# Expert outputs stored by slot and gathered afterwards, with the middle phase run one chunk per step

## The chip, the cores and the metric

The kernel runs on one core of one Trainium2 chip. The metric is the device time of one execution in microseconds. The kernel is written by hand in a language that names each engine's instructions: TensorE (PE), VectorE (DVE), ScalarE (ACT), GpSimd (POOL) and SyncE (SP), each with its own order of instructions, joined by semaphores.

## The reference

Two transformer layers over `x` of 16 x 256 tokens with 128 channels, in float32. Each has attention and then a mixture of eight experts, both modulated by shifts, scales and gates computed from a conditioning vector. The part that matters here runs from the experts of the first layer to the start of the second layer's attention:

```python
h = _layernorm(x) * (1 + cb) + sb
x = x + gb * _L0_ffn_ref(h, ...)      # 8 experts, top 2, capacity 1280 per expert
h = _layernorm(x) * (1 + ca) + sa     # second layer's modulation
# _L1_attn_ref(h): q, k, v; an importance per token, of which the top 76 keys per
# sequence are kept:
Q, K, V = x @ wq.T + bq, x @ wk.T + bk, x @ wv.T + bv
importance = (relu(x @ wi1.T + bi1) @ wi2.T + bi2)[..., 0]
_, top_idx = jax.lax.top_k(importance, k)
```

In `_L0_ffn_ref` each token goes to its two best experts, `gelu(x W1 + b1) W2 + b2`, and its output is the sum of the two results by the router's weights.

## The kernel before

The kernel is a chain of phases, each a block in which all engines run and at whose end they meet: opening, relative attention, normalization and router tables, `route_phase`, `expert_phase`, `middle_phase`, sparse attention, then the second layer's `route_phase`, `expert_phase` and `final_phase`.

**Routing.** `route_phase` (from line 1752) gives each of the 8192 (token, choice) pairs a slot, so that the pairs of one expert stand together: 71 half tiles of 128 rows, of which 62 are taken in pairs, so 31 full tiles of 256 rows and nine half tiles, 40 tiles in all (`XTILES`). It keeps the slots as integers in `slot_i`, and derives two tables by half tile: `r.token`, the token of each row, and `r.dest`, where each row's output goes in `y_dram`, which is laid out by choice and token.

**Experts** (`expert_phase`, line 1979; the first layer's has `gated` false). For each tile j:
- POOL gathers its rows of `h_dram` by an indirect DMA per half (`gather`, line 2243) into one of eight places of `x_rows`, and scatters the output rows of tile j-1 to `y_dram` by one more per half (`scatter`, line 2253). In its loop the scatter of tile j-1 stands ahead of the gather of tile j+8.
- PE, in the order first layer of j+1, turning of j+2, second layer of j: eight matmuls of 256 columns (line 2071), transposes (line 2080), sixteen matmuls of 128 columns (line 2090).
- ACT applies gelu (line 2132), copies the turned rows (line 2140) and copies the next expert's weights into a ring (lines 2109 to 2111).
- DVE adds the output bias (`finish`, line 2178) and writes `y`, a ring of four. `y_free` makes it wait until the scatter of tile j-4 has landed.
- SP loads the middle's weights (`ahead`), the gates, waits until all scatters have landed (the semaphores `stored`), and issues the rows of the first two chunks of the middle (`choice_rows`, line 1973).

**Middle** (`middle_phase`, line 1078). Tokens are taken in eight chunks of 512 (`NCH`). `got` holds both choices' rows. SP loads them from `y_dram`, two plain DMAs of 256 KB per chunk. For a chunk, in this order:
- ACT weighs the first choice's rows into PSUM (`weigh`, line 1227) and DVE adds the second choice's (line 1314) into `both`.
- POOL multiplies by the gates (`gate`, line 1144), DVE adds to `x` (line 1296) and takes the statistics (lines 1301 and 1306).
- ACT's square root (line 1231), DVE's reciprocal and shift (lines 1320 and 1322), ACT's `normalize` (line 1239).
- PE transposes (`to_columns`, line 1169) and ACT's `modulate` (line 1248) writes the chunk's columns `hT`.
- PE: hidden layer (line 1175), queries (line 1179), keys and values (line 1184), importance (line 1190), and the importance turned to columns (line 1197), with ACT's `rectify` (line 1255), `queries` (line 1259) and `importance` (line 1264), and DVE's `keys_values` (line 1328) and `rank` (lines 1335 and 1341).

The order is written out by hand: a loop of `NCH + 5` steps in which each engine takes parts of up to five different chunks, so the chunks overlap. POOL also makes the tables `before`, `head_mask` and `places` here (lines 1147 to 1158), beside its gating.

## Time and profile before

| | us |
|---|---|
| median of 3 runs | 1309.27 |
| lowest and highest | 1299.88, 1310.76 |
| the profiled execution | 1304.45 |
| its span, first to last instruction | 1302.7 |
| mean granted TensorE clock, share of full | 0.911 |

The profile is one execution. Times in its views are microseconds from the start of its span. "Busy" counts an engine's instructions, without waits, branches and the issuing of DMAs, but an indirect DMA counts on POOL, which makes its descriptors. PEld is the loading of weights, which runs beside PE. A row's bracket says how long the engine was idle before it and who released it. The releaser is inferred from semaphores. "Remote" is one for which the profile has no name. Over the whole span PE is busy 79%, DVE 61%, ACT and POOL 60%.

### The profile page before, as it was taken

How to read it: one execution, taken by the hardware profiler on the slowest of the kernel's cores; microseconds unless marked ns; L12 is line 12 of the kernel's file. 1: busy time of each engine (PE TensorE's matmuls, PEld its weight loads, DVE VectorE, ACT ScalarE, POOL GpSimd, SP SyncE). 2: the span in 40 equal slices, each digit the busy share in tenths (PEclk: the TensorE clock that was granted, in tenths of full speed). 3: DMA queues.
4: the chain of work that ended last, by engine and by line, in shares of the span. 5: the costliest groups of instructions: out<-in, count | busy, mean ns of one | idle time of the engine just before them, and what ended most of it. 6: DMA issues, size and time to landing. Idle time of an engine off the chain costs nothing. (4 is left out here: it accounts for less than half of the span.)

```text
span 1302.7 us, 40110 instructions
## 1 busy us (share of the span) xinstructions
PE 1026.4 (79%) x16123; PEld 818.8 (63%) x16123; DVE 799.8 (61%) x1631; ACT 785.2 (60%) x1734; POOL 787.2 (60%) x807
## 2 busy tenths in 40 slices
PE   6788999999999647577677477899964787899970
PEld 4467777777777536567566433566643676788860
DVE  6578788888887585000000277699967545666765
ACT  5355555555555437345446685577753777788983
POOL 7566786877867402666656320788830366788764
PEclk9789999999999977898888889799986799999995
DMA  4733232323320162111111310200037111111117
GB/s 128 166 52 54 50 57 51 57 53 57 56 45 8 19 194 53 54 44 41 43 41 39 111 42 1 70 6 7 6 67 240 54 36 35 43 42 45 39 31 200
DMA packets 120840, 79.32 MB, mean 61 GB/s; under 512 B 44144, under 2 KB 111120, under 8 KB 120528
## 3 DMA queue, kind: packets, MB, share of 16 engines
q1 hardware_dynamic: 111568, 58.12, 19.6%
q0 software_dynamic: 9088, 18.63, 4.9%
q8 instruction: 129, 2.11, 0.7%
q14 instruction: 55, 0.45, 0.1%
HBM read 58.15 MB, written 17.76 MB: 58 GB/s over the span
## 5 line engine op out<-in xcount | busy, mean ns | idle before, releaser
L2071 PE MATMUL ps_h_x_m<-x_T_x_m,fc_x_m 128*128 128x256 f32 (+1 forms) x960 | 221.2, 384 | 77.8 <-issue 51.2
L2132 ACT ACTIVATE act_x_m<-ps_h_x_m,fc_bias_x_m 128x256 f32<-128x256 f32 (+1 forms) x480 | 181.5, 464 | 137.2 <-DMA q_dram<-qT 68.5
L2071 PEld LDWEIGHTS ps_h_x_m<-x_T_x_m,fc_x_m 128*128 128x128 f32 x960 | 175.3, 205 | 106.2 <-issue 85.5
L1027 ACT ACTIVATE probT<-ps_t 128x512 f32<-128x512 f32 (+1 forms) x208 | 118.7, 594 | 145.0 <-PE ps_t L855 143.8
L2253 POOL DMA_INDIRECT y_dram<-y_x_m,dest_m x142 | 144.5, 1018 | 94.4 <-DVE y_x_m L2178 44.7
L2243 POOL DMA_INDIRECT x_rows_x_m<-h_dram,token_m x142 | 141.8, 999 | 95.5 <-POOLq L1765 56.0
L2090 PE MATMUL ps_o_x_m<-proj_x_m,act_x_m 128*128 128x128 f32 x1136 | 145.5, 280 | 12.0 <-DVE act_x_m L2156 8.5
L2090 PEld LDWEIGHTS ps_o_x_m<-proj_x_m,act_x_m 128*128 128x128 f32 x1136 | 136.8, 196 | 15.8 <-DVE act_x_m L2156 10.9
L777 POOL TENSOR_TENSOR rel_y<-rel_raw,own_rows 128x1024 f32<-128x1024 f32 x64 | 130.4, 2040 | 26.7 <-ACT rel_raw L1035 26.6
L2178 DVE TENSOR_TENSOR y_x_m<-ps_o_x_m,out_rows_m 128x256 f32<-128x256 f32 (+1 forms) x40 | 15.8, 395 | 210.7 <-remote 155.6
L957 DVE TENSOR_REDUCE neg_max<-ps_s 128x8 f32<-128x512 f32 (+1 forms) x64 | 95.5, 1492 | 73.1 <-PE ps_s L840 72.8
L855 PE MATMUL ps_t<-ident,prob 128*128 128x128 f32 x640 | 96.0, 285 | 7.7 <-ACT prob L1020 7.0
L960 DVE TENSOR_TENSOR prob<-ps_s,neg_max 128x512 f32<-128x512 f32 (+1 forms) x64 | 95.4, 1491 | 2.2
L1020 ACT ACTIVATE prob<-prob 128x512 f32<-128x512 f32 (+1 forms) x64 | 81.4, 1272 | 22.6 <-DVE prob L960 22.5
L966 DVE TENSOR_REDUCE row_sum<-prob 128x8 f32<-128x512 f32 (+1 forms) x64 | 94.4, 1475 | 0.0
L855 PEld LDWEIGHTS ps_t<-ident,prob 128*128 128x128 f32 x640 | 69.1, 142 | 25.1 <-issue 11.2
L271 POOL TENSOR_TENSOR q_rel<-q_spread,t_mask 128x2048 f32<-128x2048 f32 x16 | 73.2, 4575 | 12.8 <-DMA q_spread<-q_dram 12.8
L840 PE MATMUL ps_s<-e_rel,q_rel 64*32 64x136 f32 (+13 forms) x4096 | 74.2, 260 | 7.7 <-issue 7.7
L791 POOL TENSOR_TENSOR inv_diag<-row_inv,own_query 128x1024 f32<-128x1024 f32 x16 | 30.6, 1914 | 77.2 <-DVE row_inv L970 77.2
L2109 ACT ACTIVATE fc_x_m<-fc_all_m 128x512 f32 (+1 forms) x80 | 69.3, 866 | 7.3 <-issue 5.2
L1598 ACT ACTIVATE probT<-ps_t 128x512 f32<-128x512 f32 (+1 forms) x96 | 53.8, 593 | 29.2 <-PE ps_t L1480 28.6
L828 PE MATMUL ps_s<-kT,q_diag 32*128 32x32 f32 (+7 forms) x1024 | 56.9, 336 | 17.0 <-DVE prob L960 12.1
(316 smaller groups left out, 2133.8 us busy)
## 6 DMA issues: line engine op xcount, KB each, us to landing
q_spread<-q_dram SPq DMA_DIRECT2D x256, 64.0 KB
got_m<-y_dram SPq DMA_DIRECT2D x32, 256.0 KB, 4.7
h_dram<-h_rows_m SPq DMA_DIRECT2D x16, 256.0 KB, 2.2
x_rows_x_m<-h_dram,token_m POOLq DMA_INDIRECT x142
y_dram<-y_x_m,dest_m POOLq DMA_INDIRECT x142
x<-L_attn_x SPq DMA_DIRECT2D x8, 256.0 KB, 4.1
q_dram<-qT SPq DMA_DIRECT2D x8, 256.0 KB, 10.5
gates<-gate_dram SPq DMA_DIRECT2D x16, 128.0 KB, 4.2
```

Of the source, the lines that this page charges most:

```text
L777: pool.tensor_tensor(view(rel_y[:, u % 3, 4 * (m % 2), 0, :], 0, [[16, 4 * H], [4, 4], [1, 4]]), view(rel_raw[:, m % 3, :], 0, [[4, 4 * H] ...
L855: x = pe.transpose(ps_t[:, t % 2, p * P:(p + 1) * P], prob[:, m % 2, p, u * P:(u + 1) * P], k.ident[:, :])
L957: dve.tensor_reduce(neg_max[:, m % 2, :, :], split(ps_s[:, 0, :], m), AX.X, ALU.max, negate=True).then_inc(maxed, 1)
L960: dve.tensor_tensor(split(prob[:, m % 2, 0, :], m), split(ps_s[:, 0, :], m), view(neg_max[:, m % 2, :, :], 0, [[2, GROUPS], [1, 2], [0, n] ...
L966: dve.tensor_reduce(row_sum[:, b % 2, :, 2 * j:2 * j + 2], split(prob[:, m % 2, 0, :], m), AX.X, ALU.add).then_inc(summed, 1)
L1020: act.activation(p_, p_, ACT.Exp).then_inc(expd, 1)
L1027: act.activation(probT[to:to + n, store(m, ch), :, (2 * j + s) % 4, :], ps_t[row:row + n, t % 2, :].rearrange("p (g c) -> p g c", g=GROUPS ...
L2071: m = pe.matmul(ps_h[:, l, g, f % 2, 0:w], fc[:, slot, l, f * P:(f + 1) * P], x_T[:, slot % 2, 0:w], start=True, stop=True)
L2090: m = pe.matmul(ps_o[:, s % 2, h * P:(h + 1) * P], act1[:, s % 2, f, h * P:(h + 1) * P], proj[:, s, f, :], start=f == 0, stop=f == FK - 1)
L2132: m = act.activation(out[:, slot % 2, f, 0:w], ps_h[:, l, g, f % 2, 0:w], ACT.Tanh if l else ACT.Gelu, scale=0.5 if l else 1.0, bias=fc_bi ...
L2243: pool.indirect_dma_start(out=x_rows[:, slot, h, :], out_offset=None, in_=k.h_dram, in_offset=bass.IndirectOffsetOnAxis(ap=r.token[:, c:c ...
L2253: pool.indirect_dma_start(out=k.y_dram, out_offset=bass.IndirectOffsetOnAxis(ap=r.dest[:, c:c + 1], axis=0), in_=y[:, slot, h, :], in_offs ...
```

## The change

It does five things.

1. In the first experts POOL's scatters go. A new DRAM tensor `y_slots` holds the outputs by slot, and SP stores each tile there by a plain DMA once DVE has written it. `y_free` waits for those stores. POOL's gather of tile j+8 now waits until PE has turned tile j.
2. In the middle, POOL gathers the rows of each chunk from `y_slots` by the slots in `r.slot`, one indirect DMA per 128 tokens and choice: eight per chunk, 64 in all. SP's loads of them go, those ahead of the block's end too.
3. DVE multiplies by the gates, in place of POOL.
4. The loop of the middle has `NCH + 1` steps: in one step each engine takes chunk i from the weighing to its modulated columns, and beside it chunk i-1 from the hidden layer to the ranks.
5. POOL makes the tables at the end of the experts' phase, after the last tile is turned.

The second layer's experts and the final phase keep the scatters and the loads.

```diff
-        STEPS = NCH + 5
+        STEPS = NCH + 1
...
-        @block.sync
-        def _(sp):
-            for n in range(LEAD, NCH):
-                choice_rows(sp, k, r, n)
...
-            def gate(n):
-                pool.wait_ge(both_ready, 4 * (n + 1))
-                if n == 0:
-                    pool.wait_ge(gates_in, 16)
-                y = view(both[:, n % 2, 0, :], 0, [[2 * C, 2], [C, 2], [1, C]])
-                pool.tensor_tensor(y, y, view(gates[:, 2 * n, :], 0, [[C, 2], [0, 2], [1, C]]), ALU.mult).then_inc(gated, 1)
...
+            def choices(n):
+                for t in range(4 * n, 4 * n + 4):
+                    for c in range(TOPK):
+                        pool.indirect_dma_start(out=got[:, c, t, :], out_offset=None, in_=k.y_slots,
+                                                in_offset=bass.IndirectOffsetOnAxis(ap=r.slot[:, c * NT + t:c * NT + t + 1], axis=0)
+                                                ).then_inc(rows_in[n], 16)
+
+            for n in range(NCH):
+                choices(n)
...
             for i in range(STEPS):
-                if i == 3:
+                if i == 1:
                     pe.wait_ge(w_copied, 3)
                     pe.wait_ge(wi2_ready, 1)
-                if chunk(i - 3):
-                    hidden(i - 3)
-                    queries(i - 3)
-                if chunk(i - 2):
-                    to_columns(i - 2)
-                if chunk(i - 4):
-                    columns(i - 4)
-                if chunk(i - 3):
-                    keys_values(i - 3, 0)
-                    importance(i - 3)
-                if chunk(i - 3):
-                    keys_values(i - 3, 1)
+                if chunk(i - 1):
+                    hidden(i - 1)
+                    queries(i - 1)
+                    keys_values(i - 1, 0)
+                    importance(i - 1)
+                    keys_values(i - 1, 1)
+                    columns(i - 1)
+                if chunk(i):
+                    to_columns(i)
...
-                act.wait_ge(rows_in[n], 16 * TOPK)
+                act.wait_ge(rows_in[n], 16 * TOPK * 4)
...
-            weigh(0)
-            weigh(1)
             act.wait_ge(bq_ready, 1)
             for i in range(STEPS):
-                if chunk(i - 3):
-                    rectify(i - 3)
                 if chunk(i - 1):
-                    deviation(i - 1)
-                if chunk(i - 3):
-                    queries(i - 3)
-                if chunk(i - 2):
-                    modulate(i - 2)
+                    rectify(i - 1)
+                    queries(i - 1)
+                if chunk(i):
+                    weigh(i)
                 if chunk(i - 1):
-                    normalize(i - 1)
-                if chunk(i - 3):
-                    importance(i - 3)
-                if chunk(i + 2):
-                    weigh(i + 2)
+                    importance(i - 1)
+                if chunk(i):
+                    deviation(i)
+                    normalize(i)
+                    modulate(i)
             act.activation(warm[:, :], k.eps[:, 0:1], ACT.Exp)
 
         @block.vector
         def _(dve):
             def statistics(n):
+                dve.wait_ge(both_ready, 4 * (n + 1))
+                if n == 0:
+                    dve.wait_ge(gates_in, 16)
+                y = view(both[:, n % 2, 0, :], 0, [[2 * C, 2], [C, 2], [1, C]])
+                dve.tensor_tensor(y, y, view(gates[:, 2 * n, :], 0, [[C, 2], [0, 2], [1, C]]), ALU.mult).then_inc(gated, 1)
                 dve.wait_ge(gated, n + 1)
                 xs = k.x[:, 4 * n:4 * n + 4, :]
...
-            weigh(0)
             for i in range(STEPS):
                 if chunk(i - 1):
-                    statistics(i - 1)
-                if chunk(i - 4):
-                    keys_values(i - 4, 1)
+                    keys_values(i - 1, 0)
+                if chunk(i):
+                    weigh(i)
+                    statistics(i)
                 if chunk(i - 1):
-                    invert(i - 1)
-                if chunk(i - 5):
-                    rank(i - 5)
-                if chunk(i + 1):
-                    weigh(i + 1)
-                if chunk(i - 3):
-                    keys_values(i - 3, 0)
+                    keys_values(i - 1, 1)
+                if chunk(i):
+                    invert(i)
+                if chunk(i - 1):
+                    rank(i - 1)
...
-        slot_i, part_i = sb("slot_i", [P, KT], I32), sb("part_i", [P, 2, KT], I32)
+        slot_i, part_i = r.slot, sb("part_i", [P, 2, KT], I32)
...
+        def arrived(j):
+
+            return moved(j) if gated else count(j) if j >= 0 else 0
...
+            for j in range(0 if gated else XTILES):
+                sp.wait_ge(y_ready, j + 1)
+                c, n = first_half(j), halves(j)
+                sp.dma_start(k.y_slots[c * P:(c + n) * P, :].rearrange("(h p) c -> p h c", p=P),
+                             y[:, j % UNROLL, 0:n, :]).then_inc(stored[j % UNROLL], 16)
             for i in range(UNROLL):
-                sp.wait_ge(stored[i], 16 * moved(XTILES - 1 - (XTILES - 1 - i) % UNROLL))
-            for n in range(LEAD):
+                sp.wait_ge(stored[i], 16 * arrived(XTILES - 1 - (XTILES - 1 - i) % UNROLL))
+            for n in range(LEAD if gated else 0):
                 choice_rows(sp, k, r, n)
...
-                wait(dve, stored[j % UNROLL], 16 * moved(j - UNROLL))
+                wait(dve, stored[j % UNROLL], 16 * arrived(j - UNROLL))
...
             for j in range(XTILES + 1):
-                if not gated and exists(j - 1):
-                    scatter(j - 1)
...
-                    elif j == 0:
+                    else:
                         pool.wait_ge(x_turned, j + 1)
                         pool.nop(nofuse=True)
                     gather(j + ROWS)
                 if gated and exists(j - 1):
                     scatter(j - 1)
+            if r.tables:
+                pool.wait_ge(x_turned, XTILES)
+                pool.nop(nofuse=True)
+                r.tables(pool)
 
```

The edits left out move the table code unchanged into `middle_tables`, allocate `y_slots`, `r.slot` and the tables' tiles, and pass `tables` through.

## Rows read from the trace of the kernel before

**Rows 1.** Busy time by stretch, all engines: first experts, middle, second experts late.

```profile
core 0: us, PE busy (x) PEld busy (x) DVE busy (x) ACT busy (x) POOL busy (x), PEclk, DMA share, GB/s
508.00:536.00 28.00, 14.98 (x64) 12.24 (x64) 0.42 (x1) 10.20 (x26) 17.32 (x18) 0.70 0.36 96
536.00:660.00 124.00, 85.14 (x497) 75.49 (x497) 8.07 (x19) 59.74 (x156) 78.78 (x80) 0.87 0.15 43
...
760.00:813.00 53.00, 45.86 (x169) 22.50 (x167) 41.11 (x160) 36.70 (x80) 5.09 (x4) 0.98 0.00 1
1199.00:1233.00 34.00, 32.48 (x209) 29.57 (x208) 24.84 (x74) 30.30 (x73) 26.89 (x28) 1.00 0.13 41
...
```

**Rows 2.** Waits between 505 and 737 us: who waited for whom, total, times, longest.

```profile
DVE y_x_m L2178 <- remote: 155.6, 19, 27.5
ACT act_x_m L2132 <- DMA q_dram<-qT: 68.5, 19, 6.5
...
POOL y_dram L2253 <- DVE y_x_m L2178: 44.7, 17, 4.9
...
```

**Rows 3.** Timeline at the start of the first experts (start, us, engine, line).

```profile
521.17 1.95 PE L2090 MATMUL ps_o_x_m<-proj_x_m,act_x_m 128*128 128x128 f32 x16
...
530.40 0.94 POOL L2243 DMA_INDIRECT x_rows_x_m<-h_dram,token_m  x1 [0.30 <-issue]
...
535.01 0.42 DVE L2178 TENSOR_TENSOR y_x_m<-ps_o_x_m,out_rows_m 128x256 f32<-128x256 f32 x1 [27.45 <-remote]
...
```

**Rows 4.** Timeline, two consecutive first layers of full tiles.

```profile
594.13 1.89 PE L2071 MATMUL ps_h_x_m<-x_T_x_m,fc_x_m 128*128 128x256 f32 x8
...
597.86 1.89 PE L2071 MATMUL ps_h_x_m<-x_T_x_m,fc_x_m 128*128 128x256 f32 x8
...
```

**Rows 5.** Timeline of DVE, the outputs of tiles 1, 20, 29, 30 and 39.

```profile
536.29 0.42 DVE L2178 TENSOR_TENSOR y_x_m<-ps_o_x_m,out_rows_m 128x256 f32<-128x256 f32 x1 [0.85 <-PE ps_o_x_m L2090]
...
660.60 0.43 DVE L2178 TENSOR_TENSOR y_x_m<-ps_o_x_m,out_rows_m 128x256 f32<-128x256 f32 x1 [8.33 <-remote]
...
705.94 0.42 DVE L2178 TENSOR_TENSOR y_x_m<-ps_o_x_m,out_rows_m 128x256 f32<-128x256 f32 x1 [6.53 <-remote]
712.54 0.42 DVE L2178 TENSOR_TENSOR y_x_m<-ps_o_x_m,out_rows_m 128x256 f32<-128x256 f32 x1 [6.18 <-remote]
...
733.75 0.29 DVE L2178 TENSOR_TENSOR y_x_m<-ps_o_x_m,out_rows_m 128x128 f32<-128x128 f32 x1 [0.81 <-PE ps_o_x_m L2090]
...
```

**Rows 6.** Timeline: the second gather of the first tile, and TensorE on that tile.

```profile
510.38 0.95 POOL L2243 DMA_INDIRECT x_rows_x_m<-h_dram,token_m  x1 [0.30 <-issue]
...
512.96 0.69 PE L2080 MATMUL ps_x_x_m<-ident,x_rows_x_m 128*128 128x128 f32 x2 [7.22 <-DMA x_rows_x_m<-h_dram,token_m]
...
```

**Rows 7.** Timeline, the middle's first instructions and first chunks.

```profile
740.87 1.09 PE L1201 MATMUL ps_q<-ident,w_rows 128*128 128x128 f32 x4 [7.35 <-PEq L1988]
...
742.94 2.41 ACT L1227 ACTIVATE ps_part<-got_m,weight_m 128x128 f32<-128x128 f32 x8
...
749.74 1.65 ACT L1239 ACTIVATE normed<-x,shift,rstd 128x128 f32<-128x128 f32 x4 [0.44 <-DVE shift L1322]
...
756.43 1.94 PE L1175 MATMUL ps_i<-hT,wi_T 128*64 128x512 f32 x2 [3.88 <-ACT hT L1248]
...
```

**Rows 8.** Timeline, the middle's last chunks.

```profile
796.68 1.07 PE L1175 MATMUL ps_i<-hT,wi_T 128*64 128x512 f32 x2
...
798.85 0.69 ACT L1259 ACTIVATE qT<-ps_q,bq 128x512 f32<-128x512 f32 x1 [0.37 <-PE ps_q L1179]
...
799.43 1.01 ACT L1248 ACTIVATE hT<-ps_out,mod 128x256 f32<-128x256 f32 x2
...
802.69 1.07 PE L1175 MATMUL ps_i<-hT,wi_T 128*64 128x512 f32 x2
...
812.41 0.48 DVE L1341 SCALAR_TENSOR_TENSOR compared<-imp_row,imp_col,before 128x256 f32<-128x256 f32 x1
...
```

**Rows 9.** The page's DMA issues: KB each, median us to landing.

```profile
h_dram<-h_rows_m SPq DMA_DIRECT2D x16, 256.0 KB, 2.2
...
```

More of the change, by code:

```diff
@@ L1075, with middle_tables @@
 TINY = 2.0 ** -126
+def middle_tables(pool, a):
+    step = Chain(pool, a.table_step)
+    before = a.before
+    step(pool.memset(before[:, :, :], -TINY))
+    step(pool.affine_select(out=before[:, :, :], in_=before[:, :, :], compare_op=ALU.is_gt, fill=0.0, base=0,
+                            pattern=[[P, 2], [-1, T]], channel_multiplier=1))
+    step(pool.memset(a.head_mask[:, :], 1.0))
+    for p in range(4):
+        m = a.head_mask[4 * HD * p:4 * HD * (p + 1), :]
+        step(pool.affine_select(out=m, in_=m, compare_op=ALU.is_ge, fill=0.0, base=0,
+                                pattern=[[-HD, 4]], channel_multiplier=1))
+        step(pool.affine_select(out=m, in_=m, compare_op=ALU.is_ge, fill=0.0, base=HD - 1,
+                                pattern=[[HD, 4]], channel_multiplier=-1))
+    pool.iota(a.places[:, :], [[1, KEPT]], base=0, channel_multiplier=0,
+              allow_small_or_imprecise_dtypes=True).then_inc(a.tables_ready, 1)
 def middle_phase(nc, k, r, a):
@@ L2342, in _, with experts @@
             sp.wait_ge(stored, 16 * NCH)
-def experts(nc, d, k, name, layer, gate_w, gate_b, capacity, weights, gated, ahead, then):
+def experts(nc, d, k, name, layer, gate_w, gate_b, capacity, weights, gated, ahead, tables, then):
     with ExitStack() as ctx:
@@ L2374, in experts, with layer0_experts @@
         then(r)
-def layer0_experts(nc, d, k, ahead, then):
+def layer0_experts(nc, d, k, ahead, tables, then):
     w = Place()
@@ L2381, in layer0_experts @@
     w.rows = [d["L0_ffn_proj_bias"]]
-    experts(nc, d, k, "_m0", 0, d["L0_ffn_gate_w"], None, CAPACITY, w, False, ahead, then)
+    experts(nc, d, k, "_m0", 0, d["L0_ffn_gate_w"], None, CAPACITY, w, False, ahead, tables, then)
 def layers_between(nc, d, k):
@@ L2410, in then, with tables @@
                 middle_phase(nc, k, r, a)
-            layer0_experts(nc, d, k, ahead, then)
+            def tables(pool):
+                middle_tables(pool, a)
+            layer0_experts(nc, d, k, ahead, tables, then)
             clear_semaphores(nc, k)
```

31 lines of the change are left out of this document (10 added, 21 removed).

## The prediction, made before the changed kernel was built or run

> **What bounds the kernel now.** I read the busy time by stretch first. The first experts run from 508 to 736 us, the middle from 741 to 813 us. Between 536 and 660 us no engine is full: PE 85 of 124 us, ACT 60, POOL 79, DVE 8 [rows 1]. So the stage is held by waits, and the table of waits comes next: DVE waits 155.6 us for the second layer, under a releaser the profile cannot name, ACT 68.5 us before its activations (also under an impossible name), and POOL 44.7 us for DVE [rows 2]. POOL, whose scatters the change removes, itself waits in this stage, so its 1.0 us issues are not simply the bound.
>
> The timeline shows what is late. TensorE's 16 second-layer matmuls of tile 0 stand at 521.17 to 523.12 us, yet DVE starts on their result only at 535.01, after 27.45 us of idleness; POOL's row of gathers ended at 531.34 [rows 3]. The results of TensorE reach their readers late while POOL issues indirect DMAs back to back, and arrive together soon after POOL falls idle. In the middle, where POOL issues none, ACT's copy of the queries starts 2.17 us after the hidden layer's matmuls began, and those and the queries' own take all of it [rows 8]. That is a reading of times, not a proof. Two facts set the scale. Undisturbed, a full tile takes 597.86 - 594.13 = 3.73 us of PE [rows 4]. In fact 29 tiles take 712.54 - 536.29 = 176.3 us, or 6.08 each; between 660.60 and 705.94 nine take 5.04 each [rows 5]. POOL's four issues per full tile (two gathers, two scatters) cost 4 x 1.3 = 5.2 us: 78.78/80 = 0.98 busy each [rows 1] and 0.30 between [rows 3]. So scatters cost in two ways: they set a floor of 5.2 us, and they keep POOL busy without a break.
>
> **First experts: what the scatters' going brings.** 71 scatters leave POOL. Per full tile it has 2 x 1.25 = 2.5 us of work [rows 3, 6], under PE's 3.73. The stores go to SP, 40 plain DMAs of 64 or 128 KB. A plain store of 256 KB lands in 2.2 us [rows 9]; the output ring has four slots, some 15 us, so DVE does not wait. SP has the middle's weights and the gates ahead of them, and they are issued by 517 us, before tile 0's output exists. The added wait for x_turned before each gather binds little: POOL is eight tiles ahead.
>
> How near to 3.73 does a tile come? The nearest case is late in the second experts (1199 to 1233 us), where a tile has three indirect DMAs instead of four: PE is busy 32.48 of 34 us at full granted clock, while POOL is busy 26.89 of it [rows 1]. So with pauses in POOL's stream the lateness goes. Bounds: 3.73 (PE's own work) and 6.08 (nothing gained). I take 4.1, near the first, since some lateness may stay. The first 28 us, sixteen gathers back to back, stay as they are. Tile 1's output still ends at 536.7, then 29 x 4.1 = 118.9, then nine half tiles as before, 733.75 - 712.54 = 21.2: the last output ends at 676.8 instead of 734.04. That is -57.3 us.
>
> **Between the stages.** Before: last output 734.04, first instruction of the middle 740.84 [rows 5, 7], with a scatter, its landing and four loads issued by SP. After: a store of 2.2 us and the same barrier, about 4.5 us until POOL issues.
>
> **Middle: what comes instead.** Rows no longer arrive by eight-tile loads of 256 KB. POOL issues 64 gathers, eight per chunk, 1.25 us each with the gap: 10 us per chunk, 80 us in all. A gather begun at 510.38 is used by PE at 512.96 [rows 6], so a chunk's rows are there 7 x 1.25 + 2.6 = 11.3 us after its first issue. The first chunk pays all of it.
>
> The second half of the change sets the pace, though. Everything from weighing to the modulated columns of a chunk is now one step, and ACT weighs the next chunk only behind rectify and queries of the one before. Its length: from the first weighing (742.94) to the last normalization (751.39) is 8.45 us [rows 7]. POOL's gating of 1.3 us in it becomes a DVE operation of 0.7, leaving 7.9; transposes 0.6 and modulation 1.01 [rows 8] with hops make 9.6. Before ACT weighs again come hidden and queries matmuls and the queries copy: 796.68 to 799.54 [rows 8], with a hop 3.0 us. Period: 12.6 us, more than POOL's 10. Before, chunks overlapped over five steps at about 6.1 us (802.69 - 796.68 = 6.0 between two chunks' hidden layers [rows 8]).
>
> That is at full clock. PE's work per chunk, about 45.86/53 of the old 6.1 us [rows 1], 5.3 us, or somewhat more, is then under half of the time. Where PE was busy 15 of 28 us (508 to 536) the granted clock was 0.70, against 0.98 in the old middle, busy 46 of 53 [rows 1]. At 1.2 GHz the hidden layer's matmuls take 1.94 us instead of 1.07 [rows 7, 8], the queries' the same, the key and value copy that stands before DVE's weighing comes later and the transposes double: about +3.0, a period of 15.6. Between 12.6 and 15.6 I take 14.0.
>
> The Trainium skill (TensorE: Matmul & The Clock Gate, HAM oscillation) says that short bursts of matmuls with waits between them keep falling back to half rate. By that rule the period would be 15.6 throughout, and the sum 11 us above mine. The 0.70 row above agrees with it in part: the clock there was neither full nor half.
>
> Sum of the middle from the last output: 4.5 + 11.3 + 9.6 (0.4 more at half clock, 10.0) + 7 x 14.0 = 98 + the tail from the last chunk's hidden layer to the last rank, which took 802.69 to 812.89 = 10.2 before [rows 8] and has no other chunk beside it now, 8.7: 132.5 us. Before it was 812.89 - 734.04 = 78.9. That is +53.6 us.
>
> **What costs nothing.** The mask tables, about 4 us of POOL in the old middle, go to the end of the experts' stage, where POOL waits for PE anyway; their reader, the first rank, comes over 30 us later, and without that cover they would delay the first gather by 4 us. DVE's eight gatings, 8 x 0.7, are in the period. The second experts and the final phase keep their path.
>
> **The sum.** The profiled execution took 1304.45 us (span 1302.7), 4.8 below the median of 1309.27, within the three runs. 1304.45 - 57.3 + 53.6 = 1300.8; as the median lies higher I name 1303.
>
> **Rivals.**
> *PE's results come late in the middle too (slower).* POOL now issues 64 gathers without a break, just the pattern of 508 to 531 us [rows 3]. A chunk has three results of PE on its critical way (transposes, hidden, queries). For: the lateness stood beside unbroken gathers, with no scatter. Against: until 520 us, with PE at half clock and few matmuls, nothing was late, and the middle is sparser still. Price: 2.7 us each makes a period of 22 for the 80 us of issuing, so 2.7 chunks by then after the first; the other 4.3 at 14 give 4.5 + 80 + 60 + 8.7 = 153, +74 us, total 1321; at 5 us each (period 29) 163, +84, total 1331. It outweighs the gain from 1.2 us a chunk on. I take 1327.
> *Both at their floors (faster).* Tiles at 3.75: last output at 666.7, -67.4. Full clock in the middle: 4.5 + 11.3 + 9.6 + 88.2 + 8.5 = 122.1, +43.2. Total 1280. For: the late second experts [rows 1]. Against: the 0.70 row.
> *The experts gain nothing (the change does not do what it says).* If what holds PE is not POOL's issuing, tiles stay at 6.08 and only the middle's 54 us remain: 1356. Against it stands the late second experts.
>
> **Chances.** Forecast 0.45 (its own range 1283 to 1325), late results in the middle 0.27, both floors 0.25, no gain 0.03. The range 1268 to 1342 holds the first three with their spread. A measurement of this kernel tells about 1% from no change. Faster by over 1%: all of both floors and 0.11 of the forecast, 0.36. Slower by over 1%: 0.24 of the late results, 0.03 of no gain and 0.09 of the forecast, 0.36. Within 1%: 0.28.
>
> **What would show it.** Outputs of the first experts every 4 us and the last near 677 us; POOL idle between pairs of gathers; PE's clock near 1 there. In the middle, 64 gathers at 1.25 us, ACT's weighing every 14 us and not every 10, a granted clock near 0.75, and the last rank about 132 us after the last output. I am wrong if tiles stay above 5 us, if the middle follows POOL's 10 us, or if DVE and ACT there wait for PE long after its matmuls.

## The result, and the profile after: slower by 3.7%

The changed kernel takes 1351.8 us (median of 4 runs, 1346.4 to 1357.1) against 1304.6 us for the kernel before on the same chip (4 runs): ratio 1.037, 95% interval 1.032 to 1.042. The forecast was 1303 in a range of 1268 to 1342. The profiled execution took 1355.9 us, span 1353.8, against a span of 1302.7 before. Ratios and their intervals leave out the executions that were over 1.5% above the fastest of the same kernel.

First the busy time by stretch of the changed kernel, in the columns of [rows 1]:

```profile
core 0: us, PE busy (x) PEld busy (x) DVE busy (x) ACT busy (x) POOL busy (x), PEclk, DMA share, GB/s
536.00:660.00 124.00, 117.42 (x811) 109.21 (x811) 13.74 (x33) 96.96 (x261) 48.56 (x52) 0.95 0.24 62
...
700.00:740.00 40.00, 8.72 (x22) 4.03 (x22) 7.26 (x27) 5.62 (x14) 30.24 (x33) 0.59 0.20 52
...
780.00:820.00 40.00, 21.88 (x61) 10.33 (x60) 20.99 (x81) 16.61 (x39) 0.00 (x0) 0.71 0.00 0
820.00:860.00 40.00, 24.85 (x62) 10.98 (x61) 17.28 (x65) 15.84 (x33) 0.00 (x0) 0.73 0.00 1
```

Two opposite stories. From 536 to 660 us TensorE is busy 117.4 of 124 us, where it was 85.1 [rows 1]: the first experts now run at PE's own pace. From 700 to 740 us it is busy 8.7 of 40, ACT 5.6 and DVE 7.3. Only POOL is at work, with its gathers end to end, 30.24 us busy: one begins every 1.25 us, 0.95 of it busy and 0.30 between. That is the middle, and no other engine does much in it.

The outputs of the first experts on DVE, the first three, two in a row later, and the last (compare [rows 3, 5]):

```profile
542.95 0.42 DVE L2179 TENSOR_TENSOR y_x_m<-ps_o_x_m,out_rows_m 128x256 f32<-128x256 f32 x1 [32.89 <-remote]
543.90 0.42 DVE L2179 TENSOR_TENSOR y_x_m<-ps_o_x_m,out_rows_m 128x256 f32<-128x256 f32 x1 [0.52 <-PE ps_o_x_m L2091]
550.44 0.42 DVE L2179 TENSOR_TENSOR y_x_m<-ps_o_x_m,out_rows_m 128x256 f32<-128x256 f32 x1 [6.12 <-PE ps_o_x_m L2091]
...
565.41 0.42 DVE L2179 TENSOR_TENSOR y_x_m<-ps_o_x_m,out_rows_m 128x256 f32<-128x256 f32 x1 [3.31 <-PE ps_o_x_m L2091]
569.14 0.42 DVE L2179 TENSOR_TENSOR y_x_m<-ps_o_x_m,out_rows_m 128x256 f32<-128x256 f32 x1 [3.31 <-PE ps_o_x_m L2091]
...
673.02 0.29 DVE L2179 TENSOR_TENSOR y_x_m<-ps_o_x_m,out_rows_m 128x128 f32<-128x128 f32 x1 [0.81 <-PE ps_o_x_m L2091]
```

The first output is 7.9 us later than before (542.95 against 535.01), and soon a full tile takes 3.73 us, exactly PE's own work in [rows 4]. The last output ends at 673.31 instead of 734.04: 60.7 us gained. This is one execution: seven later kernels with the same first experts give their first output at 535.7 to 539.6 us and their last at 667.5 to 670.4, so differences of up to 7 us here are no effect of an edit.

The middle gives it back. In the table of waits, 676 to 770 us (the stretch in which POOL gathers, and 11 us more):

```profile
PE ps_out L1166 <- issue: 30.4, 2, 18.5
DVE kv L1322 <- remote: 30.3, 1, 30.3
...
DVE kv L1322 <- issue: 20.4, 2, 11.3
...
ACT hT L1242 <- issue: 19.7, 1, 19.7
PE ps_i L1172 <- ACT hT L1242: 19.6, 1, 19.6
...
ACT imp_row L1258 <- remote: 16.4, 2, 11.5
```

Single waits of 10 to 30 us, under releasers that explain nothing ("remote", "issue"). The timeline shows what three of them waited for:

```profile
705.58 1.12 PE L1187 MATMUL ps_i<-hid,wi_rep 64*128 64x512 f32 x2
...
711.44 0.69 ACT L1258 ACTIVATE imp_row<-ps_i,bi 128x512 f32<-128x512 f32 x1 [4.90 <-remote]
...
712.18 0.58 PE L1194 MATMUL ps_col<-ident,imp_row 1*128 1x1 f32 x4 [4.41 <-ACT imp_row L1258]
...
724.63 1.12 PE L1166 MATMUL ps_out<-ident,normed 128*128 128x128 f32 x4 [11.87 <-issue]
733.12 0.16 DVE L1329 COPY imp_col<-ps_col 128x4 f32<-128x4 f32 x1 [10.22 <-remote]
...
744.33 1.02 ACT L1242 ACTIVATE hT<-ps_out,mod 128x256 f32<-128x256 f32 x2 [19.75 <-issue]
```

TensorE's matmuls for the importance are over at 706.7, and ACT copies the result 4.7 us later. The four turned columns are over at 712.8 and DVE takes them at 733.1, 20 us later, though only 10.2 of these are its wait for them. The four transposes of the next chunk are over at 725.8, and ACT modulates them at 744.3, 18.6 us later. These are the late results of [rows 3], now in a stage where one chain of such results is all there is.

Two more of them stand in the way of the chunks, the keys and values:

```profile
706.63 1.13 PE L1181 MATMUL ps_kv<-w_T,hT 128*128 128x256 f32 x4
...
721.93 0.69 DVE L1322 TENSOR_TENSOR kv<-ps_kv,bkv 128x512 f32<-128x512 f32 x1 [11.29 <-issue]
...
749.16 1.03 PE L1181 MATMUL ps_kv<-w_T,hT 128*128 128x256 f32 x4
...
765.36 0.69 DVE L1322 TENSOR_TENSOR kv<-ps_kv,bkv 128x512 f32<-128x512 f32 x1 [30.25 <-remote]
```

In the one-step order DVE inverts the deviation of chunk i only behind the second half of the keys and values of chunk i-1, and adds the rows of chunk i only behind their first half. The second half, over at 707.8, is read at 721.93, after a wait of 11.3 us. The first half of the next chunk, over at 750.2, is read at 765.36, 15 us later.

The last gather ends at 759.3 us. The last late results are read at 765.4 and 768.9 (DVE's keys and values, ACT's importance), and from then on the lateness is gone. ACT on the next chunks:

```profile
785.84 1.65 ACT L1233 ACTIVATE normed<-x,shift,rstd 128x128 f32<-128x128 f32 x4 [0.56 <-DVE shift L1316]
788.70 1.02 ACT L1242 ACTIVATE hT<-ps_out,mod 128x256 f32<-128x256 f32 x2 [1.21 <-PE ps_out L1166]
```

Modulation waits 1.21 us for the transposes and chunks follow each other every 14.9 us. The eight modulations start at 699.58, 744.33, 773.76, 788.70, 803.46, 818.66, 833.47 and 848.03. So the second chunk took 44.8 us, the third 29.4, and the other five 14.9 each.

The page's groups and DMA issues for the new operations:

```profile
L1153 POOL DMA_INDIRECT got_m<-y_slots,slot_m x64 | 60.9, 952 | 26.0 <-issue 19.2
...
y_slots<-y_x_m SPq DMA_DIRECT2D x31, 128.0 KB, 1.9
```

The middle lasts 186.3 us from the last output to the last rank, which ends at 859.63; before it was 78.9. So the stage gives 107 us away for the 60.7 won. With 4 us more in the second experts (from the first gather to DVE's last reading of TensorE's output 245.6 instead of 241.7) that is the span's 51 us.

### The profile page after: what moved, and what is told of

The parts are those of the page before. It is cut to its first block and busy times, and to the rows that moved or that the text cites. A ratio compares the mean times of both kernels' runs of the same rounds, so it can differ in the third digit from the quotient of the medians.

```text
span 1353.8 us, 40121 instructions
## 1 busy us (share of the span) xinstructions
PE 1036.4 (77%) x16123; PEld 821.0 (61%) x16123; DVE 803.4 (59%) x1639; ACT 787.6 (58%) x1734; POOL 764.5 (56%) x792
## 5 line engine op out<-in xcount | busy, mean ns | idle before, releaser
L2072 PE MATMUL ps_h_x_m<-x_T_x_m,fc_x_m 128*128 128x256 f32 (+1 forms) x960 | 210.6, 371 | 25.1 <-issue 22.7
L1027 ACT ACTIVATE probT<-ps_t 128x512 f32<-128x512 f32 (+1 forms) x208 | 118.8, 594 | 146.5 <-PE ps_t L855 145.3
L2072 PEld LDWEIGHTS ps_h_x_m<-x_T_x_m,fc_x_m 128*128 128x128 f32 x960 | 169.4, 198 | 49.7 <-issue 30.9
L2254 POOL DMA_INDIRECT y_dram<-y_x_m,dest_m x71 | 72.6, 1023 | 29.6 <-issue 21.5
L1153 POOL DMA_INDIRECT got_m<-y_slots,slot_m x64 | 60.9, 952 | 26.0 <-issue 19.2
L1618 POOL TENSOR_SCALAR select<-places,rank 128x76 f32<-128x76 f32 x32 | 14.9, 479 | 102.1 <-POOLq L61 102.1
```

Source lines behind the costliest of these rows:

```text
L1027: act.activation(probT[to:to + n, store(m, ch), :, (2 * j + s) % 4, :], ps_t[row:row + n, t % 2, :].rearrange("p (g c) -> p g c", g=GROUPS ...
L2072: m = pe.matmul(ps_h[:, l, g, f % 2, 0:w], fc[:, slot, l, f * P:(f + 1) * P], x_T[:, slot % 2, 0:w], start=True, stop=True)
```

## The experiments

Theory L: while POOL issues indirect DMAs back to back, TensorE's results reach their readers late. The rivals: the one-step order of the middle is the cost (O), the middle merely waits for its rows (W), a busy POOL is enough, whatever it does (B). Kernels e1 to f4 and g1 ran once each, g2 to g4 six to ten times. All kernels are measured by three points that the timeline shows: the last output of the first experts, the last rank, and between them the middle.

**e1: the middle's rows by plain loads.** POOL's 64 gathers go, SP loads in their place.

```diff
-            for n in range(NCH):
-                choices(n)
...
+            for n in range(NCH):
+                for c in range(TOPK):
+                    first = 4 * n + c
+                    sp.dma_start(got[:, c, 4 * n:4 * n + 4, :],
+                                 k.y_slots.rearrange("(n p) c -> p n c", p=P)[:, first:first + 4, :]).then_inc(rows_in[n], 16)
```

> Edit: the changed kernel, but the middle's rows come by 16 plain loads of SP from y_slots instead of 64 gathers of POOL (so it leaves out the choice of the rows; amount and layout are the same). The one-step order and DVE's gates stay. Theory L (TensorE's results reach their readers late while POOL issues gathers back to back): no late results in the middle, weighing of the first chunk some 8 us after the last output, then 14.5 to 15 us a chunk, middle 125 to 135 us from the last output to the last rank instead of 186, total 1290 to 1300 (after is 1352). Rival O (the one-step order itself makes the middle long): middle stays at 165 us or more, total above 1330.

Measured: 1285.7 us (before 1297.4 on the same chip, one execution each), 4 under my range; the middle takes 133.3 us, within it. No result is late: "remote" releases nobody, and all eight modulations wait 1.2 us. Chunks follow every 14.8 us on average from the first to the last. O falls as the whole cause: 53.0 us of the 186.3 have gone with POOL's gathers. About 8 of these are no late result: the first modulation starts 17.9 us after the last output instead of 26.3, since the first rows come sooner. This kernel leaves out the choice of the rows, and so do e2, f2 and f3: they price a part and are no versions to use.

**e2: as e1, in the old order.**

```diff
-        STEPS = NCH + 1
+        STEPS = NCH + 5
...
-                    statistics(i)
+                    statistics(i - 1)
```

(and so on for the three engines, as the kernel before has it; DVE keeps the gates.)

> Edit: as e1, and the middle's engines in the order of the kernel before (13 steps), DVE keeps the gates. Theory L: middle about as before (79 us, up to 85 with the gates on DVE), total 1240 to 1252: the experts' gain alone, 55 to 65 us below before. Against e1 it prices the one-step order at some 50 us. Rival O would put 90 us or more between e1 and e2.

Measured: 1232.2 us, 65 us under before and 8 under the lowest I had named. The middle takes 79.6 us, as before (78.9), so DVE's gates cost nothing that shows. Against e1 the one-step order costs 53.7 us. The granted clock was lower in it; how much of the 53.7 us that makes, no run shows. The stretch 700 to 740 us of e1:

```profile
700.00:740.00 40.00, 25.39 (x63) 11.36 (x62) 17.60 (x63) 16.49 (x37) 0.00 (x0) 0.70 0.00 0
```

TensorE is busy 25.4 of 40 us at a granted clock of 0.70, against 45.9 of 53 at 0.98 in the old middle [rows 1].

So the ledger of the changed kernel's middle is: 79.6 (old order, plain rows), + 53.7 (one-step order), + 53.0 (POOL's gathers) = 186.3 us. The parts depend on the order in which they are added: by way of e3 below, the gathers are 63.6 and the one-step order 43.1.

**e3: POOL's gathers, old order.** The edit of e2 made to the changed kernel itself.

```diff
-        STEPS = NCH + 1
+        STEPS = NCH + 5
```

> Edit: the changed kernel with POOL's 64 gathers, but the middle's engines in the order of the kernel before (13 steps). If the gathers only set a pace (10 us a chunk, last rows 86 us after the last output, then the old order's tail of 25 to 30 us): middle 111 to 116, total 1277 to 1285. Theory L: late results as well, so middle 120 to 160, total 1286 to 1325, with waits on results that had long been computed in the first 80 us. Rival O: as the pace alone.

Measured: 1299.8 us; middle 143.2 us, in the range of L and 27 above the most that the pace of the gathers allows. Its modulations show it: they start at 718.30, 739.69, 764.85, then every 6 to 8 us. With these gathers the old order is no rescue; it ends level with the kernel before.

The trace of e3 also shows that theory L is too narrow. Here DVE waits late for results of its own:

```profile
719.76 0.68 DVE L1295 TENSOR_TENSOR both<-both,gates_m 128x512 f32<-128x512 f32 x1
...
726.33 0.69 DVE L1298 TENSOR_TENSOR x<-x,both 128x512 f32<-128x512 f32 x1 [5.89 <-remote]
```

The addition needs only the product, over at 720.44, and starts 5.9 us later. The next chunk has the same (6.7 us), and the moments come 4.7 us after their statistics twice. In e1, e4 and f1 none of these waits is above 0.6 us.

**e4: slower gathers.**

```diff
                 for t in range(4 * n, 4 * n + 4):
                     for c in range(TOPK):
...
+                    idle_step(pool.memset(idle[:, :], 0.0))
```

> Edit: the changed kernel, with a memset of POOL (128x1152, by the trace's memsets about 1.05 us) after each pair of gathers, so that a pair takes 3.6 us as in the first experts, where no result was late; 64 gathers then take 115 instead of 80 us. Theory L (back to back is what counts): no late results, chunks at 14.5 to 15 us, last rank about 146 us after the last output instead of 186, total 1307 to 1318: slower gathers make the kernel faster. Rival G (any gather delays results): late results over the whole 115 us, total 1352 or more. Rival O: 1345 to 1365.

POOL in e4, and the busy time of a stretch:

```profile
700.42 0.94 POOL L1157 DMA_INDIRECT got_m<-y_slots,slot_m  x1 [0.30 <-issue]
701.37 1.07 POOL L1160 MEMSET idle_p<- 128x1152 f32 x1
702.71 0.95 POOL L1157 DMA_INDIRECT got_m<-y_slots,slot_m  x1 [0.27 <-POOL idle_p L1160]
```

```profile
700.00:740.00 40.00, 24.11 (x62) 10.99 (x60) 19.42 (x73) 16.15 (x37) 33.36 (x35) 0.71 0.14 37
```

Measured: 1300.6 us, 51 below the changed kernel's median, and a middle of 144.4 us instead of 186.3. A pair of gathers takes 3.54 us, of which 1.3 are free of gathers; the same gathers take 113 us instead of 80, POOL is even busier, and TensorE does 24.1 us of work in the stretch in which it did 8.7. No wait is named "remote", and chunks follow every 14.9 us. The 11 us over e1's middle are all ahead of the first modulation (29.4 us after the last output, against 17.9), where the first rows are awaited. It is the plainest evidence for L: making the suspect slower makes the kernel faster. It was 6 us faster than the lowest I had named, 4.8 of it because the last output came at 668.5 instead of 673.3 (it stands at 667.5 to 670.4 in the seven kernels of this section with the same experts).

**f2: gathers that nobody reads.** Beside e1's plain loads POOL does this:

```diff
+        @block.gpsimd
+        def _(pool):
+            for t in range(NT):
+                if t == NT // 2:
+                    pool.wait_ge(unread_in, 16 * TOPK * t)
+                for c in range(TOPK):
+                    pool.indirect_dma_start(out=unread[:, c, t % (NT // 2), :], out_offset=None, in_=k.y_slots,
+                                            in_offset=bass.IndirectOffsetOnAxis(ap=r.slot[:, c * NT + t:c * NT + t + 1], axis=0)
+                                            ).then_inc(unread_in, 16)
```

> Edit: e1 (rows by plain loads, one-step order), and beside it POOL issues 64 gathers of the same rows, back to back, into a buffer that nobody reads (one short wait after the 32nd, since the buffer holds half). Nothing in the middle depends on them, so what they cost is what issuing them does to others. Theory L: results late again while POOL issues, middle 175 to 190 us instead of 133, total 1325 to 1345. Rival W (the changed kernel's middle waited for its rows): middle 133 to 140, total 1286 to 1293.

The waits of f2, 676 to 800 us:

```profile
DVE kv L1331 <- remote: 46.2, 3, 30.9
...
ACT hT L1251 <- remote: 19.8, 1, 19.8
...
DVE imp_col L1338 <- remote: 11.4, 2, 10.3
```

and its second chunk, TensorE's transposes and the modulation that reads them:

```profile
706.63 1.11 PE L1175 MATMUL ps_out<-ident,normed 128*128 128x128 f32 x4 [9.49 <-ACT normed L1242]
```

```profile
726.35 1.02 ACT L1251 ACTIVATE hT<-ps_out,mod 128x256 f32<-128x256 f32 x2 [19.77 <-remote]
```

Measured: 1347.1 us, 2 over my range, and a middle of 182.9 us against e1's 133.3. The rows are there as early as in e1, and nothing in the middle depends on POOL. Still the transposes, over at 707.7, are read at 726.4. W falls: gathers that nobody waits for, with the rows in place, cost 49.6 us.

**f3: a busy POOL without gathers.** Beside e1's plain loads, memsets of 128x1024:

```diff
+            for _ in range(80):
+                idle_step(pool.memset(idle[:, :], 0.0))
```

> Edit: e1, and beside it POOL does 80 memsets (128x1024, by the trace's memsets some 0.9 us each) one after the other, some 80 us, and no gather. Theory L (the issue of indirect DMAs is what delays): middle 133 to 137, total 1284 to 1291. Rival B (a busy POOL is enough): middle 160 or more, total above 1310.

The stretch 700 to 740 us, as shown of e1:

```profile
700.00:740.00 40.00, 26.54 (x66) 11.97 (x66) 16.63 (x62) 16.51 (x37) 37.70 (x41) 0.67 0.00 0
```

Measured: 1288.0 us, middle 133.0 us, the same as e1's 133.3, with POOL busy 37.7 of 40 us. B falls. It is the indirect DMAs, not POOL being busy.

Two rivals had no run of their own, but the traces bear on them. *The traffic of the gathers*: between 536 and 660 us of the changed kernel, where outputs are read on time, the DMA engines' share is 0.24 at 62 GB/s; between 700 and 740, where they are not, it is 0.20 at 52. So the amount moved is not the cause by itself; whether it is the making of the descriptors or the small packets that come without a break stays open. *Loading of the engines' code*: the trace lists the instruction queues' transfers, and there is none between 704 and 778 us of the changed kernel, nor between 695 and 770 of f2, so none of the late waits there ends on one.

**f4: the order alone, on the kernel before.**

```diff
-        STEPS = NCH + 5
+        STEPS = NCH + 1
```

STEPS and the three engines' order as in the changed kernel, gates on DVE; scatters and eight-tile loads stay.

> Edit: the kernel before, its scatters and plain loads kept, with only the middle's one-step order and the gates on DVE. Middle 131 to 136 us instead of 79 (e1 against e2 gave 53.7), total 1348 to 1356: this part of the change alone costs about what the whole change does, and theory L says that it comes without a late result. If the order is costly only where rows come late, 1300 to 1320.

Measured: 1357.9 us (before 1312.7 on the same chip), middle 133.3 us instead of 78.9, and no late result in it. The total is 2 us over my range. One part of the change, alone, costs 54 us in its stage and 45 in the total, about what the whole change costs.

**f1: the old order with short breaks.** e3, with the memset of e4 shortened to 128x256 (0.33 us, with its wait 0.6).

```diff
-        idle = sb("idle_p", [P, 1152])
+        idle = sb("idle_p", [P, 256])
```

> Edit: e3 (old order, POOL's gathers), with a short memset of POOL (128x256) after each pair of gathers, some 0.4 us with its wait, so that 64 gathers take about 93 us instead of 80. Theory L with any break being enough: no result is late; last rows 100 us after the last output, then the old order's tail, which from the last weighing to the last rank took 36 us in e3: middle 130 to 138 instead of 143, total 1285 to 1294, though the gathers are 13 us slower. If a short break does not release the results (only the share of time counts): middle 150 or more, total 1306 or more.

Measured: 1300.6 us (before 1312.7); middle 133.6 us, in the range, 9.6 below e3 though the gathers take 90 us instead of 80. No wait in it is named "remote", and while POOL gathers the modulations follow every 11.2 to 12.7 us, near the gathers' own 11.2 a chunk. The total missed its range by 7 us: the second experts, which the edit does not touch, took 247.2 us here and 236.8 in e3. That stage spreads over 231 (e2) to 247 us among the kernels e1 to f4, and single totals within 10 us of each other say nothing. That is why I compare stages.

**g1: breaks in the first experts.** The changed kernel, with the same short memset after each tile's gathers in the first experts.

```diff
+            def pause():
+                if not gated:
+                    idle_step(pool.memset(idle[:, :], 0.0))
...
             def gather(j):
...
+                pause()
```

> Edit: the changed kernel, with a short memset of POOL (128x256) after each tile's gathers in the first experts only; the middle is left as it is. In the changed kernel the first output came at 543 us though its matmuls had long ended, with the first 19 gathers issued back to back. Theory L: with breaks the first outputs come at 525 to 530 us, the last at 656 to 661 instead of 673, total 12 to 17 us below after: 1335 to 1340. If the start is set by something else than late results (the gathers' own pace, the weights): last output at 670 or later, total 1348 or more.

TensorE's second-layer matmuls of the first two tiles, and DVE's reading of them:

```profile
521.34 1.95 PE L2092 MATMUL ps_o_x_m<-proj_x_m,act_x_m 128*128 128x128 f32 x16
...
525.08 1.95 PE L2092 MATMUL ps_o_x_m<-proj_x_m,act_x_m 128*128 128x128 f32 x16
...
528.16 0.42 DVE L2180 TENSOR_TENSOR y_x_m<-ps_o_x_m,out_rows_m 128x256 f32<-128x256 f32 x1 [20.44 <-PE ps_o_x_m L2092]
...
535.55 0.42 DVE L2180 TENSOR_TENSOR y_x_m<-ps_o_x_m,out_rows_m 128x256 f32<-128x256 f32 x1 [6.96 <-remote]
```

Measured: 1344.2 us, 4 over my range, and the last output at 662.6. The first output comes at 528.16, still 4.9 us after its matmuls ended at 523.3, and the second 8.5 us after its own. So a break of 0.6 us in 2.8 shortens the lateness here and does not end it. Against the profiled execution of the changed kernel (673.3) the last output gains 10.7 us, where I had named 12 to 17; against the seven other kernels with its first experts (667.5 to 670.4) only 5 to 8. The two later kernels with these breaks (g3, g4) have it at 657.2 and 654.9. The middle, whose code is that of the changed kernel, takes 185.6 us (there 186.3).

**g2: the same breaks in the kernel before.** After each tile's gathers and after each tile's scatters, nothing of the change.

```diff
+            def pause():
+                if not gated:
+                    idle_step(pool.memset(idle[:, :], 0.0))
...
             def scatter(j):
...
+                pause()
```

> Edit: the kernel before, and nothing of the change: only a short memset of POOL (128x256) after each tile's gathers and after each tile's scatters in the first experts, 0.3 us more work for POOL each. Theory L: no result late there, so the first output comes some 8 us earlier and a full tile takes 5.6 to 5.8 us instead of 6.08: last output 12 to 22 us earlier, ratio 0.983 to 0.992. Rival P (POOL's own issue sets the tile): a tile gets 0.6 us longer, ratio 1.005 to 1.015.

The waits of g2, 505 to 737 us, and two of its outputs:

```profile
DVE y_x_m L2179 <- DMA y_dram<-y_x_m,dest_m: 159.1, 32, 6.8
```

```profile
608.96 0.43 DVE L2179 TENSOR_TENSOR y_x_m<-ps_o_x_m,out_rows_m 128x256 f32<-128x256 f32 x1 [5.86 <-DMA y_dram<-y_x_m,dest_m]
615.25 0.42 DVE L2179 TENSOR_TENSOR y_x_m<-ps_o_x_m,out_rows_m 128x256 f32<-128x256 f32 x1 [5.86 <-DMA y_dram<-y_x_m,dest_m]
```

Measured over 9 runs against 17 of before: ratio 1.000, interval 0.996 to 1.003. This forecast failed, and it is worth the most. The outputs come regularly now, every 6.29 us, and DVE waits for a free output buffer, that is for the landing of a scatter. POOL's round of two scatters, two gathers, two memsets and its waits is 6.29 us. The kernel before, with its late results, made 6.08 us on average, and POOL's four issues alone are 5.2 of these. So the breaks that end the lateness add 1.1 us to POOL's round, where I had counted 0.6, and the lateness had cost 0.9: the one eats up the other. At most 0.9 us a tile could be had while the scatters stay with POOL, since 5.2 is its floor.

**g3: a version meant to beat both.** The changed kernel with short breaks in both places and a rearranged one-step order:

```diff
-                if chunk(i - 1):
-                    keys_values(i - 1, 0)
                 if chunk(i):
                     weigh(i)
                     statistics(i)
                 if chunk(i - 1):
-                    keys_values(i - 1, 1)
+                    keys_values(i - 1, 0)
                 if chunk(i):
                     invert(i)
                 if chunk(i - 1):
+                    keys_values(i - 1, 1)
                     rank(i - 1)
```

(DVE; ACT weighs ahead of rectify and queries, and TensorE turns chunk i ahead of the second half of chunk i - 1.)

> Edit: the changed kernel with the short memsets in the first experts (g1) and after each pair of the middle's gathers (f1), and in the middle the one-step order turned so that a chunk's weighing and statistics go ahead of the keys and values of the chunk before it, and its transposes ahead of that chunk's second half. No late results: last output at 656 to 661 us, chunks at the gathers' pace of 11.2 us (12.5 if the chain does not keep up), last rank 115 to 130 us after the last output, total 1262 to 1282, ratio to before 0.966 to 0.98. If theory L did not hold for the start, 12 us more.

Measured: 1280.9 us (6 runs against 17 of before), ratio 0.986, interval 0.981 to 0.991: faster than both kernels, though less than the 0.966 to 0.98 that I had named. Last output 657.2 (expected 656 to 661), middle 134.9 us, where I had expected 130 at most. Its busy time:

```profile
536.00:660.00 124.00, 119.46 (x860) 111.38 (x859) 14.53 (x37) 100.82 (x279) 59.04 (x91) 1.00 0.24 63
...
700.00:740.00 40.00, 18.47 (x54) 9.68 (x53) 17.75 (x68) 15.28 (x35) 31.89 (x43) 0.71 0.18 46
```

Its chunks follow at 10.9 and 13.4, then at 16.4, 16.4 and 16.7 us while POOL gathers, and at 12.0 after it, with "remote" waits of 17.7 us in all before DVE's keys and values: some lateness is left, as g1 says.

**g4: breaks in the second experts too.**

```diff
-                if not gated:
+                if True:
                     idle_step(pool.memset(idle[:, :], 0.0))
```

> Edit: g3, with the short memsets also in the second experts, after each tile's gathers and after its scatters. There a tile takes 5.9 us with TensorE busy for 0.9 of it, and outputs wait for results already computed for 29 us in all (9 times, at most 5.1 us). Theory L: 3 to 12 us below g3. If POOL's longer work counts for more (two memsets of 0.3 us a tile, 40 tiles): up to 10 us above g3.

The outputs of g4's second experts, two in a row, and what they wait for between 996 and 1253 us:

```profile
1112.96 0.42 DVE L2195 SCALAR_TENSOR_TENSOR cen_x_m<-ps_o_x_m,x_rows_x_m 128x256 f32<-128x256 f32 x1
1120.02 0.42 DVE L2195 SCALAR_TENSOR_TENSOR cen_x_m<-ps_o_x_m,x_rows_x_m 128x256 f32<-128x256 f32 x1
```

```profile
DVE y_x_m L2215 <- POOL inv_std_x_m L2277: 65.0, 29, 3.5
```

Measured: 1292.4 us, ratio 0.996 (0.993 to 0.999), so 11 us worse than g3; I had leaned to the gain, and had named a loss of 10 us at most. A tile there takes 7.06 us instead of 6.10 in g3, and DVE's normalization waits for POOL's power operation 29 times. In that stage POOL's stream bounds the tile, and two memsets more in it make the tile longer. Its middle, whose code is that of g3, took 125.4 us instead of 134.9: late results strike differently from one execution to the next, so 10 us between two middles in which they strike is no effect of an edit.

| kernel | rows, order of the middle | last output | last rank | middle |
|---|---|---|---|---|
| before | plain, old | 734.0 | 812.9 | 78.9 |
| after | gathers, one step | 673.3 | 859.6 | 186.3 |
| e2 | plain, old | 670.4 | 750.0 | 79.6 |
| e1 | plain, one step | 667.5 | 800.8 | 133.3 |
| f3 | e1 + busy POOL | 667.7 | 800.8 | 133.0 |
| f2 | e1 + unread gathers | 669.9 | 852.9 | 182.9 |
| e3 | gathers, old | 669.4 | 812.6 | 143.2 |
| f1 | e3 + short breaks | 668.6 | 802.2 | 133.6 |
| e4 | after + long breaks | 668.5 | 813.0 | 144.4 |
| f4 | before, one step | 727.8 | 861.1 | 133.3 |
| g1 | after + breaks in the experts | 662.6 | 848.2 | 185.6 |
| g2 | before + breaks in the experts | 731.5 | 816.2 | 84.7 |
| g3 | breaks, rearranged | 657.2 | 792.1 | 134.9 |
| g4 | g3 + breaks in the second experts | 654.9 | 780.4 | 125.4 |

## Why the prediction was wrong, point by point

**First experts: right in size.** I had 4.1 us a full tile and the last output at 676.8, a gain of 57.3 us. Measured: 3.73 us and 673.3, a gain of 60.7. "The scatters cost in two ways" was right, but I gave the late results too large a part of the stage: of the 2.35 us that a tile took above PE's own 3.73, POOL's floor of 5.2 makes 1.5 and the late results at most 0.9, and g2 shows that ending the lateness by breaks brings nothing. The forecast held because the change removes both at once. The start did not "stay as it is" either: the first output came 7.9 us later, with the gathers unbroken to 538.8 (0.7 to 4.6 us later in the seven other kernels with these experts).

**Between the stages:** 5.8 us to the first gather, taken 4.5. **First rows:** 11.4 us, taken 11.3. **First chunk's chain:** 9.0 us, taken 10.0.

**The period of the middle: nearly right where nothing disturbs it.** I took 14.0 us between 12.6 (full clock) and 15.6 (half). It was 14.9 for the last five chunks, and 14.8 throughout e1, at a granted clock of 0.70 to 0.73: short by 4.3 us over five periods. By the rule of the Trainium skill (TensorE: Matmul & The Clock Gate, HAM oscillation), that short bursts of matmuls with waits between them keep falling back to half rate, I had worked out 15.6; the measured period stands between the two, as the granted clock stands between half and full. The tail took 11.6 us, taken 8.7. The order itself costs 53.7 us (e1 less e2). I had +53.6 for the whole middle, and that the two numbers agree is luck: mine has 11.3 us of waiting for the first rows in it, where e1 waits 8 less. What it lacked was POOL's effect on the others.

**The step that failed: seven periods of 14.0.** They took 148.5 us instead of 98. Five of them are the 4.3 us above; the other two, the second and the third chunk, took 44.8 and 29.4 us, 46.2 more than 28. That is the rival "PE's results come late in the middle too". I had seen the mechanism, had named its pattern ("64 gathers without a break, just the pattern of 508 to 531 us") and gave it 0.27, with a price of 2.7 or 5 us for each late result. The sum put it at nothing, and the rival's price was too small. Such prices are of the size of a stage average (a tile of 6.08 us is 2.35 above PE's 3.73), and there eight tiles were in flight and POOL paused whenever it waited for DVE. The right row stood in the same group: in [rows 3] a result that had ended at 523.12 was read at 535.01, some 12 us late, while gathers ran unbroken. In the middle nothing breaks the row of 64, and a chunk hangs on several results of TensorE one after the other. And "against: the middle is sparser still" had no force: f2 shows that a sparse stage is no protection.

The rival also counted the wrong results. It named the transposes, the hidden layer and the queries. The trace of after has on the chunks' way the second half of the keys and values (11.3 us of waiting) and the transposes (a wait of 19.75 us instead of 1.21, so 18.5 more) in the second chunk, and the first half of the keys and values (15 us) in the third. An undisturbed 14.9 and the first two make 44.7 us, measured 44.8; 14.9 and the third make 29.9, measured 29.4. The late importance and its columns lay beside the way. Three results at the 12 us of [rows 3] would have added 36 us to the sum, 1337 in all; that there are three, and that they average 15, is known only from the result.

**A rule that reads against the result.** All runs with unbroken gathers in the middle show results held back, TensorE's by up to 19 us, and f3 shows that it takes indirect DMAs to do so. The Trainium skill (SBUF — State Buffer, Who interferes with whom) says that TensorE and ScalarE never wait on anyone and that a DMA never contends with a compute engine. About ports that may be so; here it must not be read as "POOL's DMAs cost TensorE's readers nothing". The Trainium skill (Perfetto Trace Analysis, Per-instruction lifecycle) also says that the time in which a semaphore spreads lies outside what the profile shows of an instruction. That fits the middle, where the matmuls stand in the trace at their time and the readers are late. It does not fit all: in the first experts of the changed kernel TensorE's own stream is slow. Of tile 1's sixteen matmuls, which wait for nothing between them, some come one by one:

```profile
532.17 0.27 PE L2091 MATMUL ps_o_x_m<-proj_x_m,act_x_m 128*128 128x128 f32 x1 [0.18 <-issue]
534.99 0.37 PE L2091 MATMUL ps_o_x_m<-proj_x_m,act_x_m 128*128 128x128 f32 x1 [2.54 <-issue]
...
542.68 1.02 PE L2091 MATMUL ps_o_x_m<-proj_x_m,act_x_m 128*128 128x128 f32 x4 [0.33 <-issue]
```

And in e3 DVE waits 4.7 to 6.7 us for its own results. So what is held back is more than the message of a matmul's end. What it is, and where, stays open; ends of matmuls are modelled in the profile.

## What to carry to other kernels

Where POOL issues indirect DMAs end to end, take the delay of a single result from one pair of rows (end of the matmuls, start of the reader), not from a stage's average, and follow the order of each engine to find the results that a step waits for in series. If a stage must gather, put 1.3 us of other work or idleness into each 3.5 us of POOL's stream, as e4 does, unless POOL's stream is itself the bound, as in the second experts, where two short breaks cost 1 us a tile. And keep a deep software pipeline: folding up to five chunks' work into a step of two cost 54 us here by itself (e1 against e2, and f4).

## What the runs showed of the hardware that was not expected

- Unbroken indirect DMAs of POOL (0.95 us each, 0.30 between) delay what reads TensorE's results by 5 to 19 us (725.8 to 744.3 us in the changed kernel; 707.7 to 726.4 in f2), even when nobody needs the gathered data. In e3 they delay DVE's reading of its own results too, by 4.7 to 6.7 us.
- The delay does not start at once: in the changed kernel the gathers of the middle begin at 679.15, and all readers are on time until 706; in the kernel before they begin at 508.84, and the first results read late are those over at 521 and 523 us.
- Memsets of POOL, 37.7 of 40 us busy, delay nothing (f3: middle 133.0 us, e1 133.3).
- The delay depends on the breaks. Pairs of gathers at a pitch of 3.5 to 3.7 us: none (e4, and the first experts of the changed kernel). At 2.8 us, with 0.6 us free: from none (the middle of f1) to 4.9 and 8.5 us (g1). I have no run between 2.8 and 3.5.
- A stage with TensorE busy 24 to 25 of 40 us had a mean granted clock of 0.70 to 0.73, between the levels of 1.2 and 2.4 GHz; busy 117 of 124 us it had 0.95.
